# Span rows interleaved over the decays, constant rows laid out by the host, and h as three rounded products behind the third temporal gate

## What is computed

```
def layer0(x):                      # weights chosen by the sequence's language id
    h = relu(x @ W1 + b1)           # 512 -> 128
    y = x + h @ W2 + b2             # 128 -> 512
    return layernorm(y) * gamma + beta
def layer1(x):
    ctx = causal_ema(x, tau_ctx)
    gated = x * sigmoid([x, ctx] @ Wg.T + bg)
    mod = 0.5 + sigmoid(gelu(x @ Wn1.T + bn1) @ Wn2.T + bn2)      # 8 values per token
    traces = [causal_ema(gated * mod[:, d], tau[d]) for d in range(8)]
    temporal = sum_d traces[d] * softmax(blend)[d]
    gate = sigmoid(temporal @ Wtemp.T + btemp)
    soma = gelu(x @ Wsoma.T + bsoma)
    return layernorm((soma * gate) @ Wout.T) * gamma + beta
x = x + layer0(x);  x = x + layer1(x)
```

## Time and profile before

| what | us |
|---|---|
| median of three timed runs | 1365.72 (1363.05 to 1369.72) |
| the profiled execution | 1361.66 |
| its span | 1359.8 |
| TensorE busy | 1312.5 (97%) |
| VectorE busy | 1028.8 (76%) |
| ScalarE busy | 521.1 (38%) |
| GpSimd busy | 373.9 (28%) |
| span copies, grep<-g_blocks: median from issue to landing | 4.5 |
| xT, grep<-in_xc: the same | 10.8 |

### The profile page before, as it was taken

One profiled execution on the slowest core, in us unless ns is written; L12 is line 12 of the kernel. 1 busy time (PEld: TensorE's weight loads), 2 busy tenths in 40 slices (PEclk: granted clock), 3 DMA queues, 4 the chain that ended last, 5 costly groups with the idle time before them and its releaser, 6 DMA issues.

```text
span 1359.8 us, 19735 instructions
## 1 busy us (share of the span) xinstructions
PE 1312.5 (97%) x7908; PEld 991.4 (73%) x7908; DVE 1028.8 (76%) x1526; ACT 521.1 (38%) x822; POOL 373.9 (28%) x294
## 2 busy tenths in 40 slices
PE   4889999999999999999999999999999999999997
PEld 2657778677786867768677686777868777786766
DVE  7988677887778777677786768777787786778575
ACT  3425243443524424243343433425244252434422
POOL 4405142051411404133131422304123041421102
PEclk9999999999999999999999999999999999999999
DMA  8382542907247180561706526074451825426060
GB/s 268 130 223 88 156 154 78 240 32 207 103 116 202 70 240 31 149 200 62 218 32 175 174 78 202 32 224 124 117 169 65 232 78 156 154 79 169 36 182 32
DMA packets 91486, 186.25 MB, mean 137 GB/s; under 512 B 9858, under 2 KB 14594, under 8 KB 87298
## 3 DMA queue, kind: packets, MB, share of 16 engines
q1 hardware_dynamic: 82178, 168.20, 42.4%
q10 hardware_dynamic: 9216, 16.78, 3.7%
HBM read 134.61 MB, written 50.33 MB: 136 GB/s over the span
## 4 chain that ended last, share of the span: by engine, by line
PE 36%; DVE 23%; DMA 16%; issue 13%; ACT 6%; SPq 2%; POOL 2%; DVEq 0%; POOLq 0%
PE ring L984 26%; DVE U L863 11%; DMA grep<-g_blocks 8%; DMA g_blocks<-g_f 7%; PE ring L977 4%; SPq L355 2%; DVE x L793 2%; DVE stats L798 2%; ACT U L523 2%; DVE g_f L872 2%; PE Tp L1158 1%; PE Tp L1169 1%; DMA x<-g_blocks 1%; POOL rows L441 1%; PE ring L1183 1%
## 5 line engine op out<-in xcount | busy, mean ns | idle before, releaser
L863 DVE TENSOR_TENSOR U<-grep,w_qs 128x1024 f32<-128x1024 f32 x192 | 227.3, 1219 | 56.9 <-issue 36.7
L412 POOL TENSOR_TENSOR x<-grep,b_row 128x512 f32<-128x512 f32 x64 | 80.5, 1289 | 547.5 <-DMA grep<-in_x 547.5
L1158 PE MATMUL Tp<-U,Arep 128*32 128x256 f32 x2048 | 133.6, 385 | 13.9 <-DVE U L863 13.2
L533 ACT ACTIVATE g_f<-g_f 128x512 f32<-128x512 f32 x64 | 40.4, 632 | 259.3 <-DVE g_f L868 259.1
L425 POOL TENSOR_TENSOR grep<-grep,beta_row 128x512 f32<-128x512 f32 x64 | 82.8, 1327 | 116.7 <-DMA grep<-x_tiles 116.6
L1158 PEld LDWEIGHTS Tp<-U,Arep 128*32 128x32 f32 x2048 | 54.1, 109 | 79.3 <-DVE U L863 39.6
L868 DVE TENSOR_TENSOR g_f<-ring,bg_row 128x512 f32<-128x512 f32 x64 | 44.1, 689 | 85.2 <-PE ring L984 85.2
L984 PE MATMUL ring<-seq_hi,Wtemp_hi 128*128 128x512 f32 x256 | 106.7, 417 | 0.1
L984 PE MATMUL ring<-x1T_hi,Wsoma_hi 128*128 128x512 f32 x256 | 103.2, 403 | 0.0
L984 PE MATMUL ring<-Wg_hi,x1T_hi 128*128 128x512 f32 x256 | 103.2, 403 | 0.0
L984 PE MATMUL ring<-Wout_hi,g_r 128*128 128x512 f32 x256 | 99.8, 390 | 1.1 <-DVE soma_r L720 1.0
(11 more groups left out here) (173 smaller groups left out, 2878.8 us busy)
## 6 DMA issues: line engine op xcount, KB each, us to landing
grep<-g_blocks SPq DMA_DIRECT2D x192, 256.0 KB, 4.5
grep<-in_xc SPq DMA_DIRECT2D x16, 1024.0 KB, 10.8
grep<-in_x SPq DMA_DIRECT2D x16, 1024.0 KB, 9.0
x_tiles<-x SPq DMA_DIRECT2D x16, 1024.0 KB, 9.0
g_blocks<-g_f ACTq DMA_DIRECT2D x64, 256.0 KB, 3.8
x<-g_blocks SPq DMA_DIRECT2D x64, 256.0 KB, 5.3
grep<-x_tiles SPq DMA_DIRECT2D x16, 1024.0 KB, 4.8
out<-U SPq DMA_DIRECT2D x64, 256.0 KB, 2.0
```

Of the source, the lines that this page charges most:

```text
L412: nc.gpsimd.tensor_tensor(new[:, b, :], x_t[:, b, :], b2_row[:, :], ALU.add).then_inc(xb2_ready, 1)
L533: nc.scalar.activation(g[:, b, :], g[:, b, :], ACT.Sigmoid).then_inc(sig_ready, 1)
L863: V_.tensor_tensor(U[:, (n + 2) % 4, :, :], spans_of(k, b)[:, :, at], w_qs[:, hh, at].unsqueeze(1).to_broadcast([P, NI, HC]), ALU.mult).th ...
L1158: last = nc.tensor.matmul(Tp[b % 2][i * L:(i + 1) * L, at], Arep[:, b * NI + i, hh, :], U[:, (n + 2) % 4, i, :], start=(hh == 0 and c == 0 ...
```

## The change

- A span copy now writes partitions q, q+4, ..., q+124 in place of 32 neighbours: row 4s+q of the buffer holds place s for decay q. The decay tables, the blend weights and the masks follow (r // NQ and r % NQ for r % L and r // L).
- The modulation per row and span can no longer be spread by 16 matmuls with slices of the identity; four matmuls with a table `spread`, loaded each stage into T_sb1, put the values of all decays on each row, and VectorE keeps the row's own by a product with `own` and a sum.
- For tiles 2 to 15, h is three rounded products. ScalarE makes the high parts of W1 (in the memory of Arep) and xT (in that of U), and GpSimd the low parts, at the head of their slots. W1's are made anew for each tile.
- h stands behind the third temporal gate, relu and the parts of hid behind the third gate's as well, n1 ahead of y; the gelu of n1 waits for y, since it writes where hid_lo is.
- b2, gamma, beta and bg come from the host as 128 equal rows, not as one row that the DMA repeats.

```diff
-        grep = [sb(f"grep_{n}", [P, NI, C]) for n in range(2)]
+        grep_1, xT_lo = sb_two_ways("grep_1", [P, NI, C])
+        grep = [sb("grep_0", [P, NI, C]), grep_1]
...
-        Arep = sb("Arep", [P, NB * NI, NH, L])
+        Arep, W1_parts = sb_two_ways("Arep", [P, NB * NI, NH, L])
+        W1_split = W1_parts[:, :, :, :].rearrange("p x h t -> p (x h t)").rearrange("p (a n m) -> p a n m", a=2, n=NC)
...
-        U = sb("U", [P, 4, NI, HC])
+        U, U_rounded = sb_two_ways("U", [P, 4, NI, HC])
+        xT_hi = U_rounded[:, 0:2, :, :].rearrange("p n i c -> p (n i c)").rearrange("p (b c) -> p b c", c=C)
...
+        m_all = U[:, 3, NI - 1, 96:96 + NI * NB * D].rearrange("p (y q) -> p y q", q=NQ)
...
-                order += [("temp", k - 1, 0), ("temp", k - 1, 1)]
+                order += [("temp", k - 1, e) for e in range(NC - 1)]
             if has_next and k != 0:
                 order += [("h", k + 1, 0)]
             if has_prev:
-                order += [("temp", k - 1, 2), ("temp", k - 1, 3)]
+                order += [("temp", k - 1, NC - 1)]
...
-                sp.dma_start(b2_row[:, :], b2[bass.ds(one, 1)].to_broadcast([P, C])).then_inc(ld_b2, 16)
+                sp.dma_start(b2_row[:, :], b2[bass.ds(one, 1)].rearrange("a p m -> p (a m)")).then_inc(ld_b2, 16)
...
+                sp.dma_start(own_q, own).then_inc(ld_small, 16)
...
+                def load_spread():
+                    if has_next:
+                        sp.wait_ge(full["y"], upto(4, k + 1, NB - 1))
+                    else:
+                        sp.wait_ge(full["tt"], upto(4, k - 1, NB - 1))
+                    sp.dma_start(T_sb1[:, :], spread).then_inc(ld_spread, 16)
...
                     for q in range(NQ):
-                        sp.dma_start(spans_of(k, b)[q * L:(q + 1) * L, :, :],
+                        sp.dma_start(spans_of(k, b)[q:P:NQ, :, :],
...
                     sp.dma_start(x1_back[:, :, :].rearrange("p b c -> p (b c)"), x1_dram[(k - 1) & 1]).then_inc(ld_back, 16)
+                    if has_cur:
+                        load_spread()
                     for b in range(NB):
                         sp.wait_ge(res_ready, upto(4, k - 1, b))
                         sp.dma_start(out_tiles[k - 1, b * P:(b + 1) * P, :], res[:, b, :]).then_inc(stored, 16)
                 else:
                     second_loads()
+                    load_spread()
...
+                if has_next and k >= 1:
+                    pool.wait_ge(w1hi_ready, k)
+                    nc.gpsimd.tensor_tensor(W1_split[:, 1, :, :], W1[:, :, :], W1_split[:, 0, :, :].bitcast(F),
+                                            ALU.subtract).then_inc(w1lo_ready, 1)
+                    for n in range(NC):
+                        pool.wait_ge(xThi_ready, upto(4, k - 1, n))
+                        nc.gpsimd.tensor_tensor(xT_lo[:, n, :], xT[:, n, :], xT_hi[:, n, :].bitcast(F),
+                                                ALU.subtract).then_inc(xTlo_ready, 1)
...
+                if has_next and k >= 1:
+                    act.wait_ge(full["Uused"], upto(PIECES // 2, k - 1, PIECES // 2 - 1))
+                    if k & 1:
+                        act.wait_ge(ld_w1, 32 * ((k + 1) // 2 + 1))
+                    nc.scalar.activation(W1_split[:, 0, :, :], W1[:, :, :], ACT.Identity).then_inc(w1hi_ready, 1)
+                    act.wait_ge(ld_xT, 16 * upto(1, k + 1, 0))
+                    for n in range(NC):
+                        nc.scalar.activation(xT_hi[:, n, :], xT[:, n, :], ACT.Identity).then_inc(xThi_ready, 1)
...
-                    if k != 0:
-                        hidden_high(k + 1)
                 if has_prev:
                     soma_gated(2)
+                if has_next and k != 0:
+                    hidden_high(k + 1)
+                if has_prev:
...
                     act.wait_ge(full["n1"], upto(1, k, 0))
+                    if has_next:
+                        act.wait_ge(full["y"], upto(4, k + 1, NB - 1))
                     nc.scalar.activation(hid[:, :], inner_bank[:, :], ACT.Gelu, bias=col[:, 0:1]).then_inc(h1_ready, 1)
...
-                    V_.tensor_copy(m_rep.rearrange("p (b i) h -> p b i h", b=NB),
-                                   smp[:, 32:32 + NI * NB * NH].rearrange("p (i b h) -> p b i h", i=NI, b=NB)).then_inc(mrep_ready, 1)
+                    V_.tensor_tensor(m_all, smp[:, 32:32 + NI * NB * D].rearrange("p (y q) -> p y q", q=NQ),
+                                     own_q.unsqueeze(1).to_broadcast([P, NI * NB * NH, NQ]), ALU.mult).then_inc(mall_ready, 1)
+                    dve.wait_ge(mall_ready, upto(1, k, 0))
+                    V_.tensor_reduce(m_rep.rearrange("p (b i) h -> p i b h", b=NB),
+                                     m_all.rearrange("p (i b h) q -> p i b h q", i=NI, b=NB), AX.X, ALU.add).then_inc(mrep_ready, 1)
...
                     pe.wait_ge(ld_xT, 16 * upto(1, tile, 0))
-                    if tile % 2 == 0:
-                        pe.wait_ge(ld_w1, 32 * (tile // 2 + 1))
-                    product(ps[:, :], lambda n: W1[:, n, :], lambda n: xT[:, n, :], NC, "h")
+                    if tile < 2:
+                        if tile == 0:
+                            pe.wait_ge(ld_w1, 32)
+                        product(ps[:, :], lambda n: W1[:, n, :], lambda n: xT[:, n, :], NC, "h")
+                    else:
+                        pe.wait_ge(xThi_ready, upto(4, tile - 2, NC - 1))
+                        for n in range(NC):
+                            nc.tensor.matmul(ps[:, :], W1_split[:, 0, n, :], xT_hi[:, n, :], start=(n == 0), stop=False)
+                        pe.wait_ge(w1lo_ready, tile - 1)
+                        for n in range(NC):
+                            nc.tensor.matmul(ps[:, :], W1_split[:, 1, n, :], xT_hi[:, n, :], start=False, stop=False)
+                        for n in range(NC):
+                            pe.wait_ge(xTlo_ready, upto(4, tile - 2, n))
+                            last = nc.tensor.matmul(ps[:, :], W1_split[:, 0, n, :], xT_lo[:, n, :], start=False,
+                                                    stop=(n == NC - 1))
+                        last.then_inc(full["h"], 1)
...
                 if has_prev:
-                    temporal_gate(0)
-                    temporal_gate(1)
+                    for e in range(NC - 1):
+                        temporal_gate(e)
                 if has_next and k != 0:
                     hidden(k + 1)
                 if has_prev:
-                    temporal_gate(2)
-                    temporal_gate(3)
+                    temporal_gate(NC - 1)
+                if has_prev and has_cur:
+                    modulation_begun()
...
                 def spread_modulation():
 
                     pe.wait_ge(m_ready, upto(1, k, 0))
+                    pe.wait_ge(ld_spread, 16 * upto(1, k, 0))
                     for i in range(NI):
-                        for q in range(NQ):
-                            last = nc.tensor.matmul(smp[q * L:(q + 1) * L, 32 + 8 * i:40 + 8 * i], ident[:, i * L:(i + 1) * L],
-                                                    U[:, 3, NI - 1, q:NB * D:NQ], start=True, stop=True)
+                        last = nc.tensor.matmul(smp[:, 32 + NB * D * i:32 + NB * D * (i + 1)], T_sb1[:, i * P:(i + 1) * P],
+                                                U[:, 3, NI - 1, 0:NB * D], start=True, stop=True)
                     last.then_inc(full["mrep"], 1)
...
-    d = t[None, :] - (r % L)[:, None]
+    d = t[None, :] - (r // NQ)[:, None]
...
+        "x": c(xs), "xc": c(xs.transpose(0, 2, 1)), "own": (rows[:, None] % NQ == np.arange(NQ)[None, :]).astype(np.float32),
+        "spread": (np.arange(NI * P)[None, :] // NQ == rows[:, None]).astype(np.float32),
```

55 lines of the change are left out of this document (31 added, 24 removed).

## The result

The changed kernel takes 1345.91 us (median of 4 runs, 1343.37 to 1356.86), the kernel before 1364.51 (1363.05 to 1369.72): ratio 0.9877, 95% interval 0.9847 to 0.9907, 18.6 us faster by the medians. The ratio is an estimate of its own and not the quotient of the medians, which would be 0.9864; by the ratio and its interval the gain is 13 to 21 us. I had said 1348.5 us. Measured again in the last group of experiments it was 1343.08 against 1367.75, ratio 0.9825 (0.9802 to 0.9848).

The account below looks back on a forecast made before the run. TensorE, busy 97% of the span, was taken as the bound, with waits for VectorE's spans behind slow copies. Terms -10.1 - 11.9 - 2.4 + 6.4 + 0.5 = -17.5 us gave 1348.2, stated as 1348.5; range 1341 to 1361.

Parts of the forecast that it names:

- h, -10.1: TensorE, tiles 2 to 15: 12 rounded products replace four float32 matmuls, 0.72 us less per tile, -10.1 us.
- part 4: Interleaved rows: span copies write partitions q, q+4, ..., q+124; bounds 0 if the rate stays, and -18 us.
- Pre-work hidden: ScalarE's roundings and GpSimd's subtractions before h end before TensorE needs them, if xT is there; no cost.
- h starves: Rival: xT landing after 3.3 us into odd stages delays h's third group, from 4 us the first gate; 5%.
- That rival's price: With xT 5 us into odd stages, some 2 us lost in each of seven: 1348.2 + 14 = 1362 us.
- Order, 0: TensorE: h behind the third gate and n1 ahead of y are the same products in another order; cost 0.
- Copies, -11.9 - 2.4: Faster span copies make stages 1 to 14 like 3 and 12, the shortest: -11.9 us; stages 0 and 15: -2.4.
- The sentence of the Trainium skill: Taken to the letter, 32 interleaved rows gain nothing: the rival that copies get no faster, 1362.5 us, 13%.
- Spread, +6.4: Four full-weight matmuls replace sixteen small ones on TensorE: +0.34 to +0.50 us per tile, 0.40 taken, +6.4 us.
- Host rows 0: Loads of b2, gamma and beta as 128 equal rows: if anything faster, xT lands earlier, 0 to TensorE.
- start +0.5: At the start one more small load among those VectorE's first instruction waits for; issue 0.43 us, +0.5 us.
- part of which may be this very wait: Range term: the 4 us by which timed runs exceed the profile, perhaps partly TensorE's wait behind VectorE's spans.

Follow-up runs that it names:

- h alone: Kernel before plus only the three rounded h products, their preliminary work and the new order; old copies, spread and rows: 1361.5 us, ratio 0.9963.
- late xT: Changed kernel with b2, gamma and beta as repeated rows and xT loaded behind x: 1350.3 us, ratio 0.9875 to the kernel before.
- scattered stores: Two runs: changed kernel with g stored to row s*4+i, with one copy per block 1473.1 us, with four interleaved copies 1482.3 us.
- New copies alone: Kernel before with only the span copies interleaved, tables as before: 1355.5 us, ratio 0.9914.
- copies by i: Changed kernel with each block's four copies cut by span row i, each writing all 128 partitions: 1343.9 us, ratio 0.9843 to the kernel before.
- the repeat: The changed kernel itself, measured again in the last group of experiments: 1343.1 us, ratio 0.9825 to the kernel before.

## Why the prediction was right

**Sum.** -17.5 us was forecast, -18.6 measured, and -24.7 the second time. The first is the better match by luck in part, as the terms show.

*h, -10.1:* right in mechanism and size, 10.0 less work on TensorE for h alone. What I did not see is that the gain depends on part 4: alone it is worth 4.9 us, with fast copies 8.3 to 11.1.

*Pre-work hidden:* right, and its three times of day (3.9, 8 and 10.0 us into the stage) held within 0.2. The point at which h starves was wrong: "if it lands after 3.3 us" should have been close to 5. I let five subtractions wait for xT, but the one of W1 does not; and the last block of the third group is read 0.7 us after the group begins. The late xT showed 4.1 us free and 5.4 costing 0.6. That rival's price was then misplaced as well: the 7 us came mostly outside h.

*Order, 0:* no gap at h, n1 or y in the stages shown. It had no run of its own.

*Copies, -11.9 - 2.4:* the mechanism was right (224 to 309 GB/s, VectorE's wait 15.2 to 4.0 us), the size too large. I took it that the rate would be 370 and that all stages would become like 3 and 12 with their waits gone; stages of a kind still differ by 1.1 to 1.3 us, not by 0.5. Of 15.4 us of waits half went, 7.6. Stage 15 is 0.5 shorter and stage 1 begins 0.6 sooner, but over the traces of all kernels here the one takes 75.4 to 77.8 us (without the scattered stores) and the other begins at 102.3 to 112.9, so these two are within the scatter. Timed, the copies are worth 10.9 us alone and 7.8 to 10.6 in the changed kernel. What is left fits the slower issue: a block still takes 6.1 to 7.1 us from its first issue to its last landing (medians by block, longest 8.0; before 6.6 to 7.4, longest 9.3), not 2.8, and four issues 0.65 us apart are part of that. The stage's first block is no faster at all, 6.7 us in both, and VectorE waits for it in every stage. That a quicker issue would win this back was not shown, since none of the forms had one without the scattered store.

*The sentence of the Trainium skill* that I weighed there (SBUF — State Buffer, Can I just issue two DMAs to hit both halves?: "the only way to hit all 16 ports is one transfer spanning all 128 partitions") does not hold here if it is taken to the letter, as a limit on the rate: copies of 32 partitions, interleaved, ran at 309 GB/s and did as well as copies over all 128.

*Spread, +6.4:* +0.33 to 0.35 us per stage, at the low end of my bounds, 5.6 in all; since the waits behind it shrink, 0.3 to 3.1 in time.

*Host rows 0, start +0.5:* the first right in two runs; the second too small to be seen in that scatter.

So by the profiles of stages 1 to 14: 10.0 for h, 7.6 for waits, and 4.8 back for the spread, 12.8, and the stages are 13.25 shorter; the spans differ by 14.4. **The 4 to 10 us beyond that** in the timed runs had no term. The mean granted clock is 0.991 to 0.992 in the timed runs of the kernel before (three measurements, 37 runs) and 0.995 in both series of the changed kernel. 0.0035 of 1350 is 4.7 us. I had put the distance between timed runs and profile into the range as "part of which may be this very wait". Where those runs lose their clock can't be seen, since only one run of each series has a trace. In the traces stretches of a low clock stand between 20 and 54 us in all, and again between 79 and 94 us in some (h alone, row below, 0.66 with TensorE busy 8.7 of 10 us), in stage 0.

```profile
80.00:90.00 10.00, 8.72 (x60) 4.46 (x60) 7.68 (x10) 3.20 (x4) 0.00 (x0) 0.66 0.83 215
```

New copies alone had 0.993 and h alone 0.993, so no single part brings it, and the changed kernel kept 0.995 or 0.996 without the new copies, without the rounded h and without the new spread, so no single one of these carries it either. It stays open.

## What to carry to other kernels

When small transfers keep the DMA engines full at half the rate of the others, look at which partitions they write: spreading the same bytes over all of them gave over a third more rate (309 in place of 224 GB/s). The copy itself is one line, but it turns the rows of the buffer, and the tables and the spread have to follow. When an engine's work is cut ahead of a wait that another resource sets, price the two together; h alone brought half of its gain in time, and by the profile gave 8 of 10 us back at the spans. And before a DMA view is rearranged, look at its outermost dimension: four there in place of 128 left the store of g at a DMA share of 0.24.

## What was not expected of the hardware

- Interleaved copies are dearer to issue: 0.65 us from one copy of four to the next against 0.47 or less. For a block that is 2.5 in place of some 1.8 us, 0.7 of the 1.3 us that the rate gives (1049 KB at 309 in place of 224 GB/s). The copies by i, over all 128 partitions, took 2.50 us as well, so the interleaving of the destination is not the only form that is dear.
- A store with an outermost dimension of 4 ran at a share of 0.24 and 72 GB/s and cost 139 us per run, with TensorE's clock at half for some 7 us of each stage, behind its wait.
- In the profiled run of the repeat (1356.7 us), VectorE's subtraction for W2 in stage 1 took 12.60 us. In the changed kernel's first profile its eight instances took 1.47 to 1.65 us (second fence: least, median, most, in ns). TensorE's y waited 10.03 us for what lies behind it (third fence), and the clock fell to 0.50, where it still stood from 130 to 134 us.

```profile
114.38 12.60 DVE L777 TENSOR_TENSOR W_r<-W_f,W_hi 128x512 fp32r<-128x512 f32 x1
```
```profile
L777 DVE TENSOR_TENSOR W_r<-W_f,W_hi x8: 1470/1514/1645, 17.7 to 1089.6; 128x512 fp32r<-128x512 f32 x8
```
```profile
130.18 0.80 PE L1026 MATMUL ring<-W_hi,T_sb_r 128*128 128x512 f32 x1 [10.03 <-DVE T_sb_r L763]
```

It ended at 126.98, and GpSimd's queue of additions without a gap, which it had begun into, ended at 126.43:

```profile
111.53 5.07 POOL L439 TENSOR_TENSOR x<-grep,b_row 128x512 f32<-128x512 f32 x4
116.51 5.04 POOL L446 TENSOR_TENSOR grep<-grep,beta_row 128x512 f32<-128x512 f32 x4
121.47 4.96 POOL L452 TENSOR_TENSOR grep_f<-grep_f,beta_row 128x512 f32<-128x512 f32 x4
```

The Trainium skill (SBUF — State Buffer, Who interferes with whom) says that a VectorE instruction with two inputs in SBUF contends with a GpSimd instruction that reads SBUF. W2's subtraction is of that kind. VectorE's products at 110.47 and 112.41 us, with an input in PSUM (L756), took their usual 0.67 and 0.69 us beside GpSimd's work. The rule names the pair and not the length: in the changed kernel's first profile the same subtraction took 1.50 us (at 115.46) beside the same kind of GpSimd work, so it does not tell 1.5 us from 12.6. No run took GpSimd's work away here, so that GpSimd is the cause is argued and not shown, and why it happens in one trace of the changed kernel and not in the other isn't known. In none of the other 13 traces is an instruction 4 us longer than the median of its kind. Three of the changed kernel's 11 runs lie at 1356 to 1357 us, the others at 1341 to 1347; whether the other two had the same event can't be seen.
